# Eight stages without GpSimd's drain, one sort whose scatters are waited for once, and 57 of them in the gate instead of 60

## The chip, the cores and the metric

The kernel runs on one core of a Trainium2 chip. The metric is the device time of one execution in microseconds (us); lower is better. Five engines have programs of their own: PE (TensorE), DVE (VectorE), ACT (ScalarE), POOL (GpSimd) and SP (SyncE, which here only starts transfers).

## The reference, cut to what matters

The reference is a graph network of two layers over 3125 nodes of 256 features and 50,000 edges. Each layer adds to `x` a graph attention, a linear attention and an expert block:

```python
edge_index = jnp.stack([src, dst])
xn = _layernorm(x, axis=-1)
x = x + _L0_gnn_ref(xn, edge_index, edge_weight, ...) + _L0_mix_ref(xn[None], ...)[0]
x = x + _L0_ffn_ref(_layernorm(x, axis=-1)[None], ...)[0]      # 16 experts, 2 for each node
xn = _layernorm(x, axis=-1)
x = x + _L1_gnn_ref(xn, edge_index, ...) + _L1_mix_ref(xn[None], ...)[0]
x = x + _L1_ffn_ref(_layernorm(x, axis=-1)[None], ...)[0]      # 8 experts, 2 for all nodes
```

The graph attention of the first layer sums over the edges of a source node, that of the second over the edges of a destination node. So the edges are needed in two orders, and the kernel sorts them twice.

## The kernel before, in words

The kernel is eight stages, one after the other. Each stage is a function that opens one `nc.Block()`, in which every engine has a program, and closes it: `stage_project0` (p0), `stage_edges0` (e0), `stage_gate` (g), `stage_experts` (x), `stage_combine` (c), `stage_project1` (p1), `stage_edges1` (e1) and `stage_ffn1` (f). Nothing of a stage starts before all engines have ended the one before it. Names of tiles in the profile begin with the letter of the stage (`x_w` is `w` of `stage_experts`), and things that outlive a stage begin with `keep_` or `mid_`.

**What stands at a boundary.** In the compiled program the end of a block is this: PE, DVE, ACT and SP each drain (wait until their engine is idle) and report to a semaphore; GpSimd drains too, then waits for the four reports, and releases all. Then `Memory.release_semaphores` (L254 in the profile is its barrier) clears the semaphores of the stage, on GpSimd: a second drain, marked as a reset of this range of semaphores (`is_reset_sema`; the reset drain below), and the clear itself. A second barrier, of semaphores alone, follows. Then each engine branches to its program of the next stage.

**The two sorts.** An edge goes to its place by an indirect DMA of GpSimd: one DMA (a "scatter") takes one column `t` of the records, 128 edges, and writes each edge's record to the row of DRAM that `row` names. There are `EC` = 391 columns, so 391 scatters in a sort. `scatter_records` issues them in runs of `RUN` = 4 on two semaphores in turn; from the third run on a run waits until the last run on the same semaphore has landed, and at the end it waits until all have landed. The first sort (`sorted0`, records of four numbers) is wholly in p0, and e0 reads it. The second (`sorted1`, records of two) is read only by e1, and is cut in three: columns 0 to 59 (`SCATTERS_GATE` = 60) on GpSimd in g, where it has nothing else to do; columns 60 to 229 (`SCATTERS_EARLY` = 230) in x, behind the 50 scatters that send the rows of the nodes to their experts (L1321); columns 230 to 390 in p1. Each of the three calls has its own two semaphores, and ends with the wait for its own scatters.

**Orders within the stages.** In g, DVE works through normalising, the logits, the two best experts of each node and their places; its last instruction is L154, which writes `keep_expert_of`. In x, SP first loads the second weights (`x_w`, L215), then waits for the 50 scatters of GpSimd (`s_sent`), and only then loads the first tiles of rows (L1348). In e0 SP reads the sorted records first (L846); GpSimd's gathers (L863) need them. In e1 it is the same (L2097, L2120). GpSimd has no DMA in f.

Of the kernel before, what the change touches and what calls it, by code (L numbers as in the profile page):

```python
# [27 lines left out]
EC = -(-NE // P)  # L28
# [17 lines left out]
R1 = 4  # L46
assert R1 * TN >= G1_BINS
RUN = 4
SCATTERS_GATE = 60
SCATTERS_EARLY = 230  # L50
NOWHERE = 200.0

# [177 lines left out]
def scatter_records(pool, to, row, record, s_scat, begin, end):  # L230


    for n, t in enumerate(range(begin, end)):
        run = n // RUN
        if run >= 2 and n % RUN == 0:
            pool.wait_ge(s_scat[run % 2], 16 * RUN * (run // 2))
        pool.indirect_dma_start(  # L237
            out=to, out_offset=bass.IndirectOffsetOnAxis(ap=row[:, t:t + 1].bitcast(U32), axis=0),
            in_=record[:, t, :], in_offset=None).then_inc(s_scat[run % 2], 16)
    for half in range(2):  # L240
        pool.wait_ge(s_scat[half], 16 * sum(n // RUN % 2 == half for n in range(end - begin)))


class Memory:
# [32 lines left out]
def stage_project0(nc, a, k):  # L277
# [5 lines left out]
    with ExitStack() as ctx:  # L283
        m = Memory(nc, ctx, "p0")
# [86 lines left out]
        s_scat = [m.sem(f"scattered{i}") for i in range(2)]  # L371
# [28 lines left out]
        s_mixd = m.sem("mix_kept")  # L400
        s_v = m.sem("vector_steps")
        s_a = m.sem("scalar_steps")
        block = ctx.enter_context(nc.Block())

        @block.sync
        def _(sp):
# [31 lines left out]
        @block.gpsimd  # L438
        def _(pool):
            nc.gpsimd.iota(k["iota"][:], [[1, P]], base=0, channel_multiplier=0,  # L440
                           allow_small_or_imprecise_dtypes=True).then_inc(s_const, 1)
            nc.gpsimd.iota(iota_g[:], [[1, G1_N]], base=0, channel_multiplier=0,
                           allow_small_or_imprecise_dtypes=True).then_inc(s_const, 1)
            nc.gpsimd.iota(k["number"][:], [[0, 1]], base=0, channel_multiplier=1,
                           allow_small_or_imprecise_dtypes=True).then_inc(s_const, 1)
            nc.gpsimd.memset(k["ident"][:], 0.0).then_inc(s_const, 1)
            nc.gpsimd.memset(k["before"][:], 1.0).then_inc(s_const, 1)
            nc.gpsimd.memset(k["one"][:], 1.0).then_inc(s_const, 1)
            nc.gpsimd.iota(k["pairs"][:], [[1, TOPK * TN]], base=X_N * P - NP * TOPK * TN, channel_multiplier=TOPK * TN
                           ).then_inc(s_pad, 1)  # L450
            pool.wait_ge(s_const, 6)
            nc.gpsimd.affine_select(out=k["ident"][:], in_=k["ident"][:], compare_op=ALU.not_equal, fill=1.0, base=0,
                                    pattern=[[-1, P]], channel_multiplier=1).then_inc(s_const, 1)

            nc.gpsimd.affine_select(out=k["before"][:], in_=k["before"][:], compare_op=ALU.is_ge, fill=0.0, base=-1,
                                    pattern=[[1, P]], channel_multiplier=-1).then_inc(s_const, 1)
            nc.gpsimd.memset(zrow[:], 0.0).then_inc(s_pad, 1)

            pool.wait_ge(s_rows, 1)
            pool.wait_ge(s_fill, 64)  # L460
            scatter_records(pool, k["sorted0"], row0, record0, s_scat, 0, EC)

        @block.scalar
        def _(act):
# [317 lines left out]
def stage_edges0(nc, a, k):  # L782
# [7 lines left out]
    with ExitStack() as ctx:  # L790
        m = Memory(nc, ctx, "e0")
# [47 lines left out]
        s_agg = m.sem("added_up")  # L839
        s_acc = m.sem("accumulated")  # L840
        s_v = m.sem("vector_steps")
        block = ctx.enter_context(nc.Block())

        @block.sync
        def _(sp):
# [208 lines left out]
def stage_gate(nc, a, k):  # L1054


    with ExitStack() as ctx:
        m = Memory(nc, ctx, "g")
# [42 lines left out]
        s_base = m.sem("bases")  # L1101
        s_col = m.sem("bin_starts")
        s_row = m.sem("bin_starts_turned")
        s_scat = [m.sem(f"scattered{i}") for i in range(2)]
        s_v = m.sem("vector_steps")
        block = ctx.enter_context(nc.Block())

        @block.sync
        def _(sp):
# [3 lines left out]

        @block.gpsimd
        def _(pool):
            scatter_records(pool, k["sorted1"], k["row1"], k["record1"], s_scat, 0, SCATTERS_GATE)

        @block.scalar
        def _(act):
# [138 lines left out]
def stage_experts(nc, a, k):  # L1258
# [3 lines left out]
    with ExitStack() as ctx:  # L1262
        m = Memory(nc, ctx, "x")
# [27 lines left out]
        s_y = m.sem("y_made")  # L1291
        s_yk = m.sem("y_kept")
        s_out = [m.sem(f"tile_out{i}") for i in range(2)]
        s_scat = [m.sem(f"scattered{i}") for i in range(2)]
        block = ctx.enter_context(nc.Block())


        def turns(eng, step):
# [18 lines left out]
        @block.gpsimd  # L1317
        def _(pool):
            for r in range(TOPK):
                for t in range(TN):  # L1320
                    pool.indirect_dma_start(  # L1321
                        out=k["expert_in"], out_offset=bass.IndirectOffsetOnAxis(
                            ap=k["pairs"][:, r * TN + t:r * TN + t + 1].bitcast(U32), axis=0),
                        in_=k["all_rows"][:, t, :], in_offset=None).then_inc(s_sent, 16)


            scatter_records(pool, k["sorted1"], k["row1"], k["record1"], s_scat, SCATTERS_GATE, SCATTERS_EARLY)

        @block.sync
        def _(sp):  # L1330
# [119 lines left out]
def stage_combine(nc, a, k):  # L1450


    with ExitStack() as ctx:
        m = Memory(nc, ctx, "c")
# [13 lines left out]
        s_std = [m.sem(f"std{n}") for n in range(2)]  # L1468
        s_back = m.sem("scales_ready")
        s_v = m.sem("vector_steps")  # L1470
        block = ctx.enter_context(nc.Block())

        def columns(u):
            return range(u * TB, (u + 1) * TB)
# [124 lines left out]
def stage_project1(nc, a, k):  # L1599


    with ExitStack() as ctx:
        m = Memory(nc, ctx, "p1")
# [71 lines left out]
        s_num = m.sem("numerators")  # L1675
        s_att = m.sem("attention_rows")
        s_o = m.sem("outputs")
        s_scat = [m.sem(f"scattered{i}") for i in range(2)]
        s_v = m.sem("vector_steps")
        block = ctx.enter_context(nc.Block())  # L1680

        def row_of(t3, t):
            return t3[:, bass.ds(t, 1), :].rearrange("p a d -> p (a d)")
# [28 lines left out]
        @block.gpsimd  # L1712
        def _(pool):

            nc.gpsimd.memset(same[:], 1.0).then_inc(s_same, 1)
            view = same[:].rearrange("p (h d) -> p h d", h=HC)
            pool.wait_ge(s_same, 1)
            nc.gpsimd.affine_select(out=view, in_=view, compare_op=ALU.is_ge, fill=0.0, base=0,
                                    pattern=[[-MD, HC], [0, MD]], channel_multiplier=1).then_inc(s_same, 1)
            pool.wait_ge(s_same, 2)  # L1720
            nc.gpsimd.affine_select(out=view, in_=view, compare_op=ALU.is_ge, fill=0.0, base=MD - 1,
                                    pattern=[[MD, HC], [0, MD]], channel_multiplier=-1).then_inc(s_same, 1)

            scatter_records(pool, k["sorted1"], k["row1"], k["record1"], s_scat, SCATTERS_EARLY, EC)

        @block.scalar
        def _(act):
# [248 lines left out]
def stage_edges1(nc, a, k):  # L1976
# [7 lines left out]
    with ExitStack() as ctx:  # L1984
        m = Memory(nc, ctx, "e1")
# [78 lines left out]
        s_done = m.sem("averaged")  # L2064
        s_out = m.sem("written")
        s_v = m.sem("vector_steps")
        block = ctx.enter_context(nc.Block())

        def turns(eng, step, tail=(), enter=None, leave=None):

# [350 lines left out]
def stage_ffn1(nc, a, k, out):  # L2421


    with ExitStack() as ctx:
        m = Memory(nc, ctx, "f")
# [59 lines left out]
        s_res = m.sem("result_rows")  # L2485
        s_out = m.sem("written")
        s_v = m.sem("vector_steps")
        block = ctx.enter_context(nc.Block())

        def row_of(t3, t):  # L2490
            return t3[:, bass.ds(t, 1), :].rearrange("p a d -> p (a d)")
# [251 lines left out]
def build(nc, a, out):  # L2743

    with ExitStack() as ctx:
        def keep(name, shape, dt=F32):
            return ctx.enter_context(nc.sbuf_tensor(f"keep_{name}", shape, dt))

        def dram(name, shape):
            return nc.dram_tensor(f"mid_{name}", shape, F32, kind="Internal").ap()  # L2750

        k = {
            "x": keep("x", [NP, TN, D]),
            "iota": keep("iota", [P, P]),
            "number": keep("number", [P, 1]),
# [24 lines left out]
        with nc.sbuf_tensor("acc0", [P, TN, ROW], F32) as acc0:  # L2780
# [8 lines left out]
            with ExitStack() as layer:  # L2789
# [3 lines left out]
                stage_combine(nc, a, k)  # L2793
                stage_project1(nc, a, k)
        stage_edges1(nc, a, k)
        stage_ffn1(nc, a, k, out)

# [24 lines left out]
```

## Time and profile before

| | us |
|---|---|
| median of 3 runs | 3174.46 (3174.05 to 3175.06) |
| span of the profiled execution, first to last instruction | 3163.5 |
| median less span | 11.0 |
| stages (start of the first transfer of SP): e0, g, x, c, p1, e1, f | 638.93, 1246.13, 1343.95, 1720.44, 1824.03, 2137.26, 2867.91 |
| GpSimd busy | 1822.0 (58% of the span) |

The profile gives no time of the profiled execution beside its span; what lies around the span is taken as the 11.0 us between it and the median of the runs. Drains, barriers and waits are not counted as busy and have no rows of their own: they are seen as the distance from the last row of a stage to the first of the next. Times of rows are us from the start of the span.

### The profile page before, as it was taken

The numbers are of one execution on the slowest core, as the hardware profiler recorded it, in microseconds if no ns is written. First come the engines' busy times: TensorE is split into PE (matmuls) and PEld (weight loads), VectorE is DVE, ScalarE is ACT, GpSimd is POOL, SyncE is SP. The second block draws the span as 40 slices with busy tenths as digits, with TensorE's granted clock in tenths as the row PEclk, the third lists the DMA queues.
The fourth block names the chain that finished last, engine by engine and source line by source line (L and its number), as shares of the span: only waits on it lengthen the run. The fifth ranks groups of instructions, "written<-read, shape, count | busy, mean of one in ns | idle before, by whom it ended". The sixth has DMA issues, their size and how long they took to land. (4 is left out here: it accounts for less than half of the span.)

```text
span 3163.5 us, 53056 instructions
## 1 busy us (share of the span) xinstructions
PE 1683.1 (53%) x12473; PEld 1233.8 (39%) x12474; DVE 1885.3 (60%) x5563; ACT 816.7 (26%) x2575; POOL 1822.0 (58%) x1835
## 2 busy tenths in 40 slices
PE   0387544046666665409996078533444444321697
PEld 0154333035444443406664056422443334321465
DVE  6776799177777776402221922686777777665422
ACT  0144110024444442103332133001333333221232
POOL 0577777757777775677741477507777777710000
PEclk9998666568888875559998588765566656655899
DMA  3200000053333345053333200007444444842100
GB/s 111 97 22 18 2 1 2 2 194 106 106 103 106 106 102 54 1 204 82 86 85 104 60 18 17 11 0 139 105 104 106 105 105 104 86 40 81 30 16 24
DMA packets 169828, 225.16 MB, mean 71 GB/s; under 512 B 77729, under 2 KB 129096, under 8 KB 169639
## 3 DMA queue, kind: packets, MB, share of 16 engines
q0 software_dynamic: 74752, 140.02, 20.3%
q1 hardware_dynamic: 95012, 84.45, 9.2%
q8 instruction: 20, 0.33, 0.0%
q14 instruction: 44, 0.36, 0.0%
HBM read 185.16 MB, written 39.18 MB: 71 GB/s over the span
## 5 line engine op out<-in xcount | busy, mean ns | idle before, releaser
L2120 POOL DMA_INDIRECT e_rows<-mid_table,e_rec x488 | 487.8, 1000 | 258.1 <-issue 137.4
L237 POOL DMA_INDIRECT mid_sorted<-p_record,p_row x391 | 404.2, 1034 | 224.8 <-issue 122.4
L863 POOL DMA_INDIRECT e_rows<-mid_table,e_rec x448 | 433.9, 969 | 157.8 <-issue 99.0
L237 POOL DMA_INDIRECT mid_sorted<-keep_record,keep_row x391 | 396.6, 1014 | 145.9 <-issue 122.8
L1023 PE MATMUL e_ps_A<-e_rows,e_hot 128*125 128x260 f32 x896 | 329.8, 503 | 0.0
L2376 PE MATMUL e_ps_mT<-keep_ident,e_marked 128*128 128x128 f32 x488 | 118.3, 424 | 198.9 <-DVE e_marked L2144 198.9
L1023 PEld LDWEIGHTS e_ps_A<-e_rows,e_hot 128*125 128x125 f32 x896 | 202.2, 250 | 28.1
L2338 ACT ACTIVATE e_acc<-e_state 128x66 f32 x488 | 126.1, 258 | 259.3 <-ACT e_acc L2338 217.0
L1008 PE MATMUL e_ps_T<-e_identb,e_hot 128*125 128x128 bf16 x454 | 89.5, 289 | 191.4 <-DVE e_hot L884 190.2
L1384 DVE COPY x_hidden<-x_ps_h 128x512 f32<-128x512 f32 x64 | 44.2, 691 | 230.3 <-PE x_ps_h L1413 230.3
L2376 PEld LDWEIGHTS e_ps_mT<-keep_ident,e_marked 128*128 128x128 f32 x488 | 95.7, 223 | 203.4 <-issue 203.4
L2144 DVE TENSOR_TENSOR e_marked<-e_hot,e_rows 128x1024 f32<-128x1024 bf16 x61 | 74.8, 1225 | 156.9 <-DMA e_rows<-mid_table,e_rec 156.7
L904 DVE TENSOR_TENSOR e_rows<-e_rows 128x512 f32<-128x512 f32 x224 | 153.1, 684 | 1.7 <-ACT e_rows L988 1.4
L1413 PE MATMUL x_ps_h<-w,x_xT 128*128 x256 | 129.7, 630 | 14.7 <-ACT x_xT L1362 14.5
L1008 PEld LDWEIGHTS e_ps_T<-e_identb,e_hot 128*125 128x125 bf16 x454 | 53.5, 166 | 211.6 <-DVE e_hot L884 210.3
L2171 DVE SCALAR_TENSOR_TENSOR e_state<-e_state,e_scale,e_ps_A 128x65 f32<-128x65 f32 x488 | 134.9, 277 | 0.7 <-issue 0.2
L1429 PE MATMUL x_ps_y<-x_w,x_hT 128*128 x512 | 122.3, 382 | 1.7 <-ACT x_hT L1369 1.7
L137 DVE TENSOR_TENSOR_SCAN p_running<-p_ones,p_first,p_mask 128x391 f32<-128x391 f32 x125 | 118.8, 1012 | 5.3 <-DVE p_mask L134 5.3
L980 ACT ACTIVATE acc<-e_state 125x260 f32 x224 | 94.0, 420 | 101.6 <-DVE e_state L912 100.7
L884 DVE TENSOR_SCALAR e_hot<-keep_iota,e_rec 128x125 f32<-128x125 f32 x454 | 116.1, 353 | 1.1
L1429 PEld LDWEIGHTS x_ps_y<-x_w,x_hT 128*128 128x128 f32 x512 | 95.9, 190 | 45.0 <-issue 31.3
L777 PE MATMUL p_ps_mix<-p_kw,p_qvT 128*125 128x256 f32 x100 | 51.0, 664 | 115.7 <-DVE keep_x L689 114.7
(520 smaller groups left out, 4078.6 us busy)
## 6 DMA issues: line engine op xcount, KB each, us to landing
e_rows<-mid_table,e_rec POOLq DMA_INDIRECT x936
mid_expert_in<-p_zrow SPq DMA_DIRECT2D x1, 8192.0 KB
w<-in_L_ffn_w SPq DMA_DIRECT2D x16, 512.0 KB
x_w<-in_L_ffn_w SPq DMA_DIRECT2D x16, 512.0 KB
x_xs<-mid_expert_in SPq DMA_DIRECT2D x64, 128.0 KB
x_b<-in_L_ffn_b SPq DMA_DIRECT2D x64, 128.0 KB
mid_expert_out<-x_y SPq DMA_DIRECT2D x64, 128.0 KB
mid_sorted<-p_record,p_row POOLq DMA_INDIRECT x391
```

The costliest lines, as they stand in the source:

```text
L137: o.done(o.eng.tensor_tensor_scan(runnings[:, j], one, masks[:, j], first[:, bass.ds(b + j, 1)], ALU.mult, ALU.add))
L237: pool.indirect_dma_start(out=to, out_offset=bass.IndirectOffsetOnAxis(ap=row[:, t:t + 1].bitcast(U32), axis=0), in_=record[:, t, :], in_o ...
L863: pool.indirect_dma_start(out=rows[:, s % RING * 2 + j, :], out_offset=None, in_=k["table"], in_offset=bass.IndirectOffsetOnAxis(ap=rec[:, ...
L904: nc.vector.tensor_tensor(r, r, spread(w, P, 2, H, HD), ALU.mult).then_inc(s_wm, 1)
L1008: last = nc.tensor.transpose(ps_T[q % 2][0:NP, j, 0:P], halves[:, :, 1], identb[:])
L1023: last = nc.tensor.matmul(ps_A[0:NP, q % 4, 0:ROW], hot[:, q * 2 + j, :], rows[:, q * 2 + j, :], start=j == 0, stop=j == 1)
L1413: last = nc.tensor.matmul(ps_h[q % 2][:], xT[:, q % 2, c, :], k["w1"][:, bass.ds(e, 1), c, :].rearrange("p a f -> p (a f)"), start=c == 0, ...
L1429: last = nc.tensor.matmul(ps_y[q % 2][:], hT[:, c, :], w2[:, bass.ds(e, 1), c, :].rearrange("p a d -> p (a d)"), start=c == 0, stop=c == F ...
L2120: pool.indirect_dma_start(out=rows[:, j, q, :], out_offset=None, in_=k["table1"], in_offset=bass.IndirectOffsetOnAxis(ap=rec[:, i * TG + q ...
L2171: v.scalar_tensor_tensor(state[:, j, q, 0:W1], before, scale[:, j, q:q + 1], sums_of(j)[:, q // HALF, q % HALF * W1:(q % HALF + 1) * W1], ...
L2338: nc.scalar.activation(acc[:, bass.ds(block_of, 1), :].rearrange("p a w -> p (a w)"), state[:, j, q, :], ACT.Copy).then_inc(s_keep, 1)
L2376: last = nc.tensor.transpose(ps_mT[:, q // HALF, q % HALF * P:(q % HALF + 1) * P], marked[:, q, :], k["ident"][:])
```

## The change

Three things are done. All eight blocks are opened with `no_gpsimd_drain=True`: the other engines drain as before, GpSimd does not, and the barrier is the one of semaphores alone. The two semaphores of the second sort are allocated once for the whole kernel (`k["s_scat1"]`) and cleared at its very end, with one more barrier; a run is counted by the column, `t // RUN`, so that the counts go on from stage to stage, and the wait for all scatters (`scatters_landed`) stands only behind the last part, in p1. The first sort keeps its wait in p0. And the gate gets 57 scatters, so the experts' stage gets 173 where it had 170.

```diff
-SCATTERS_GATE = 60
+SCATTERS_GATE = 57
...
 def scatter_records(pool, to, row, record, s_scat, begin, end):
-    for n, t in enumerate(range(begin, end)):
-        run = n // RUN
-        if run >= 2 and n % RUN == 0:
+    for t in range(begin, end):
+        run = t // RUN
+        if run >= 2 and t % RUN == 0:
             pool.wait_ge(s_scat[run % 2], 16 * RUN * (run // 2))
         pool.indirect_dma_start(
...
+def scatters_landed(pool, s_scat):
     for half in range(2):
-        pool.wait_ge(s_scat[half], 16 * sum(n // RUN % 2 == half for n in range(end - begin)))
+        pool.wait_ge(s_scat[half], 16 * sum(t // RUN % 2 == half for t in range(EC)))
...
# in each of the eight stages:
-        block = ctx.enter_context(nc.Block())
+        block = ctx.enter_context(nc.Block(no_gpsimd_drain=True))
...
# stage_project0
             scatter_records(pool, k["sorted0"], row0, record0, s_scat, 0, EC)
+            scatters_landed(pool, s_scat)
...
# stage_gate
-            scatter_records(pool, k["sorted1"], k["row1"], k["record1"], s_scat, 0, SCATTERS_GATE)
+            scatter_records(pool, k["sorted1"], k["row1"], k["record1"], k["s_scat1"], 0, SCATTERS_GATE)
...
# stage_experts
-            scatter_records(pool, k["sorted1"], k["row1"], k["record1"], s_scat, SCATTERS_GATE, SCATTERS_EARLY)
+            scatter_records(pool, k["sorted1"], k["row1"], k["record1"], k["s_scat1"], SCATTERS_GATE, SCATTERS_EARLY)
...
# stage_project1
-            scatter_records(pool, k["sorted1"], k["row1"], k["record1"], s_scat, SCATTERS_EARLY, EC)
+            scatter_records(pool, k["sorted1"], k["row1"], k["record1"], k["s_scat1"], SCATTERS_EARLY, EC)
+            scatters_landed(pool, k["s_scat1"])
...
# build
+        s_scat1 = [nc.alloc_semaphore(f"keep_scattered{i}") for i in range(2)]
...
         stage_ffn1(nc, a, k, out)
+        nc.clear_and_free_semaphores(s_scat1)
+        nc.all_engine_barrier(sem_only=True)
```

## Rows read from the trace of the kernel before

**Rows 1.** The page's first line.
```profile
span 3163.5 us, 53056 instructions
```

**Rows 2.** The chain that ended last, its first piece: start, us, what.
```profile
2867.91 0.27 SPq L2498
```

**Rows 3.** Timeline, p0 to e0: start, us, engine, line, what, idle before.
```profile
562.62 0.36 DVE L694 CAST keep_row<-p_running 128x391 int32<-128x391 f32 x1
...
631.11 0.96 POOL L237 DMA_INDIRECT mid_sorted<-p_record,p_row  x1 [0.30 <-issue]
638.93 0.37 SPq L846 DMA_DIRECT2D e_rec<-mid_sorted  x1
...
646.41 0.99 POOL L863 DMA_INDIRECT e_rows<-mid_table,e_rec  x1 [14.34 <-DVE e_rec L917]
```

**Rows 4.** Timeline, g to x.
```profile
1332.24 0.95 POOL L237 DMA_INDIRECT mid_sorted<-keep_record,keep_row  x1 [0.30 <-issue]
...
1333.99 0.21 DVE L154 TENSOR_SCALAR keep_expert_of<-g_ps_T 1x66 int32<-1x66 f32 x1 [0.47 <-PE g_ps_T L163]
...
1336.03 0.96 POOL L237 DMA_INDIRECT mid_sorted<-keep_record,keep_row  x1 [0.30 <-issue]
1343.95 0.29 SPq L1331 DMA_DIRECT2D x_beta<-in_L_ffn_beta  x1
...
1344.63 0.96 POOL L1321 DMA_INDIRECT mid_expert_in<-acc,keep_pairs  x1 [7.65 <-POOLq L254]
```

**Rows 5.** Timeline, e0 to g.
```profile
1244.59 0.42 ACT L980 ACTIVATE acc<-e_state 125x260 f32 x1 [1.23 <-DVE e_state L912]
1246.13 0.37 SPq L215 DMA_DIRECT2D g_gw<-in_L_ffn_gate_w  x1
...
1246.80 1.00 POOL L237 DMA_INDIRECT mid_sorted<-keep_record,keep_row  x1 [23.04 <-POOLq L254]
```

**Rows 6.** Timeline, the four later boundaries.
```profile
1721.15 0.97 POOL L1498 DMA_INDIRECT c_yk<-mid_expert_out,keep_pairs  x1 [94.66 <-PEq L1453]
...
1820.32 2.56 ACT L1514 ACTIVATE acc<-keep_x,c_back,c_rstd 125x256 f32<-125x256 f32 x5 [0.46 <-DVE c_back L1576]
...
1823.55 0.20 POOL L1715 MEMSET p_same<- 128x128 f32 x1 [39.14 <-POOLq L254]
...
2129.62 6.82 DVE L1877 TENSOR_TENSOR keep_x<-keep_x,acc 125x6400 f32<-125x6400 f32 x1
2137.26 0.37 SPq L2097 DMA_DIRECT2D e_rec<-mid_sorted  x1
...
2142.88 7.70 POOL L2120 DMA_INDIRECT e_rows<-mid_table,e_rec  x1 [108.05 <-DVE e_rec L2227]
...
2779.69 1.02 POOL L2120 DMA_INDIRECT e_rows<-mid_table,e_rec  x1 [0.30 <-issue]
```

**Rows 7.** DMA traffic, 630 to 638 us, in 40 slices of 0.2 us.
```profile
GB/s 7 4 0 0 0 0 3 7 0 0 0 0 0 11 0 0 0 0 0 0 0 0 0 0 0 0 0 0 0 0 0 0 0 0 0 0 0 0 0 0
```

**Rows 8.** The same, 1334 to 1342 us.
```profile
GB/s 0 0 0 0 0 5 0 0 0 0 0 4 1 0 0 0 0 2 3 0 0 0 0 0 0 0 0 0 0 0 0 0 0 0 0 0 0 0 0 0
```

**Rows 9.** Timeline, the end of the sends in x and what waits for them.
```profile
1406.61 0.96 POOL L1321 DMA_INDIRECT mid_expert_in<-acc,keep_pairs  x1 [0.30 <-issue]
...
1409.84 0.35 SPq L1348 DMA_DIRECT2D x_xs<-mid_expert_in  x1
...
1413.61 0.66 PE L1406 MATMUL x_ps_x<-keep_ident,x_xs 128*128 128x128 f32 x2 [79.66 <-DMA x_b<-in_L_ffn_b]
```

**Rows 10.** DMA traffic there, 1404 to 1411 us, in 40 slices of 0.175 us.
```profile
GB/s 0 23 374 328 24 0 0 0 0 351 351 47 0 0 0 0 304 304 141 0 0 0 0 187 351 211 0 0 0 0 1 5 0 0 0 0 0 0 6 194
```

**Rows 11.** What is known of the scatters' landing (view of the tile `mid_sorted`).
```profile
DMA to landing us min/median/max: 2.1/2.1/5.6
```

**Rows 12.** Timeline of g: two of the scatters that took longer.
```profile
1248.10 7.33 POOL L237 DMA_INDIRECT mid_sorted<-keep_record,keep_row  x1 [0.30 <-issue]
...
1324.14 2.38 POOL L237 DMA_INDIRECT mid_sorted<-keep_record,keep_row  x1 [0.30 <-issue]
```

More of the change, by code:

```diff
@@ L841, in stage_edges0 @@
         s_v = m.sem("vector_steps")
-        block = ctx.enter_context(nc.Block())
+        block = ctx.enter_context(nc.Block(no_gpsimd_drain=True))
         @block.sync
@@ L1103, in stage_gate @@
         s_row = m.sem("bin_starts_turned")
-        s_scat = [m.sem(f"scattered{i}") for i in range(2)]
         s_v = m.sem("vector_steps")
-        block = ctx.enter_context(nc.Block())
+        block = ctx.enter_context(nc.Block(no_gpsimd_drain=True))
         @block.sync
@@ L1293, in stage_experts @@
         s_out = [m.sem(f"tile_out{i}") for i in range(2)]
-        s_scat = [m.sem(f"scattered{i}") for i in range(2)]
-        block = ctx.enter_context(nc.Block())
+        block = ctx.enter_context(nc.Block(no_gpsimd_drain=True))
         def turns(eng, step):
@@ L1470, in stage_combine @@
         s_v = m.sem("vector_steps")
-        block = ctx.enter_context(nc.Block())
+        block = ctx.enter_context(nc.Block(no_gpsimd_drain=True))
         def columns(u):
@@ L1677, in stage_project1 @@
         s_o = m.sem("outputs")
-        s_scat = [m.sem(f"scattered{i}") for i in range(2)]
         s_v = m.sem("vector_steps")
-        block = ctx.enter_context(nc.Block())
+        block = ctx.enter_context(nc.Block(no_gpsimd_drain=True))
         def row_of(t3, t):
@@ L2066, in stage_edges1 @@
         s_v = m.sem("vector_steps")
-        block = ctx.enter_context(nc.Block())
+        block = ctx.enter_context(nc.Block(no_gpsimd_drain=True))
         def turns(eng, step, tail=(), enter=None, leave=None):
@@ L2487, in stage_ffn1 @@
         s_v = m.sem("vector_steps")
-        block = ctx.enter_context(nc.Block())
+        block = ctx.enter_context(nc.Block(no_gpsimd_drain=True))
         def row_of(t3, t):
@@ L2750, in dram @@
             return nc.dram_tensor(f"mid_{name}", shape, F32, kind="Internal").ap()
+        s_scat1 = [nc.alloc_semaphore(f"keep_scattered{i}") for i in range(2)]
         k = {
+            "s_scat1": s_scat1,
             "x": keep("x", [NP, TN, D]),
```

## The prediction

> **What bounds the kernel now.** The span is 3163.5 us [rows 1]. The chain of waits begins only at 2867.91 [rows 2]: it doesn't reach back over the last boundary, so it tells nothing of this change. I read the boundaries in the timeline instead, for at each the whole chip stands still. The question at each is which engine came last, and how long after it the next stage began.
>
> At five of the seven boundaries GpSimd had long been done. From e0 to g ACT ends last, at 1244.59 + 0.42 = 1245.01, and SP starts at 1246.13, 1.12 us later; GpSimd, which idled 23.04 us, starts at 1246.80 [rows 5]. From c to p1 ACT ends at 1822.88 and GpSimd starts at 1823.55, 0.67 us later, after 39.14 us idle. From p1 to e1 DVE ends at 2136.44 and SP starts 0.82 us later. At the start of c GpSimd had idled 94.66 us; its last gather of e1 ends at 2780.71, 87 us before f [rows 2, 6]. So a boundary in which GpSimd came early costs 0.7 to 1.1 us, with both barriers, the reset drain and the clear in it.
>
> At two boundaries GpSimd comes last. In p0 DVE is done at 562.98, GpSimd's last scatter ends at 631.11 + 0.96 = 632.07, and SP starts at 638.93: 6.86 us of nothing [rows 3]. In g DVE is done at 1333.99 + 0.21 = 1334.20, the last scatter ends at 1336.99, and SP starts at 1343.95, 6.96 us after it and 9.75 after DVE [rows 4]. The two distances are the same, though 391 scatters stand behind the one and 60 behind the other. Each is three things: the last scatter lands, GpSimd drains, the barriers pass.
>
> **How much of the 6.86 is the drain.** The barriers are 1.12 [rows 5]. Landing: the last traffic of p0 lies in the fourteenth slice, 632.6 to 632.8, then nothing moves [rows 7]; in g the last lies at 1337.4 to 1337.8 and then nothing [rows 8]. So the data is down 0.7 us after GpSimd's row ends. The semaphore comes later. A neighbour says how much: the last send ends on GpSimd at 1407.57 [rows 9], its data moves until about 1408.55 [rows 10], and SP, which waits for it, loads at 1409.84, after reading the tile's expert [rows 9]. That is 1.3 us from data to the load, of which I estimate 0.4 for SP's reading: 0.9. By this the scatter has landed 0.7 + 0.9 = 1.6 us after its row, and the drain is 6.86 - 1.6 - 1.12 = 4.1 us. Bounds: data alone, 0.7, gives 5.0; the median landing of 2.1 [rows 11], counted from the row's end, gives 3.6.
>
> Here the trace goes against a rule. No byte moves from 632.8 to 638.93, and yet the chip stands [rows 7]. The Trainium skill (PSUM — Partial Sum Buffer, "Engine vs sequencer instructions") says that a drain waits for the engine to go fully idle. By that alone a drain behind a wait for everything that GpSimd issued would be free, and the first boundary would gain nothing; its time is worked out below from rows, as the first rival.
>
> **The change, part by part.**
> *The drain goes at p0 to e0.* The wait for the landing stays, so only the drain's 4.1 us go (3.6 to 5.0). Everything of e0 hangs on the barrier: SP's load of the records, then GpSimd's first gather at 646.41 [rows 3]. All of it moves up.
>
> *At g to x drain and wait go, and three scatters.* The 57th scatter starts at 1332.24 and ends at 1333.19 [rows 4], 1.0 us before DVE. Without landing and drain GpSimd is at the barrier first, and DVE sets the end: 1334.20 + 0.82 (DVE last, as at p1 to e1 [rows 6]) = 1335.0 in place of 1343.95. That is 8.9 us; by the 1.12 of rows 5 it is 8.6. I take 8.8. What could spoil it is the pace of the scatters. Two of g's long ones are 7.33 and 2.38 us [rows 12], where DVE was at work; if GpSimd fell 2.1 us further behind (two such short stalls), it would end at 1335.3 and the gain would be 7.5. So 7.5 to 9.1.
> The 8.8 carries on. In x GpSimd's 50 sends start 0.68 us after SP [rows 4], SP loads rows only when they have landed, and PE waits 79.66 us for that [rows 9]; weights and sends all hang on the barrier and move together.
>
> *Three more scatters in x* are 3 x 1.26 us (1332.24 to 1336.03 for three [rows 4]) = 3.8 us on GpSimd, queued behind the sends. They are covered by the 94.66 us that GpSimd idles at the end of x [rows 6]; without this cover they would cost their 3.8. The waits inside the runs now count by column: column 60, the fourth of x, waits for runs that were issued before 50 sends. Cost nothing. The same holds in p1, where GpSimd idles some 100 us at the end [rows 6].
>
> *The drain goes at the other six block ends.* It ran while GpSimd idled 23 us or more [rows 5, 6], and in f GpSimd has no DMA. Nothing, within 0.1 us each.
>
> *The last clear and barrier* are new, behind the last block: something like half a boundary. A whole one is 0.67 to 1.12 [rows 5, 6]; I take 0.5 us, with 0 and 1.1 as bounds.
>
> Sum: -4.1 - 8.8 + 0.5 = -12.4 us. The profiled execution would go from 3163.5 to 3150.6 in span, with the last clear outside it. Its own time is the span plus the 11.0 around it, 3174.5, the median; so 3174.5 - 12.4 = **3162.1 us**. Bounds: -(3.6 + 7.5) + 1.1 = -10.0, and -(5.0 + 9.1) = -14.1, so 3160.4 to 3164.5.
>
> **The rivals.**
> *1. The drain is cheap, the landing long.* This is the rule above as a mechanism. The longest known landing is 5.6 us [rows 11]; behind the last scatter it would reach 637.67, and 1.12 for the barriers gives 638.79, almost SP's start. Then the first boundary gains 0.1 us. The second still gains 8.8, since its wait for landing goes too. Total -0.1 - 8.8 + 0.5 = -8.4: 3166.1 us. Against it: twice the same distance, where landing is 2.1 in the median.
>
> *2. The reset drain takes over, at every boundary (slower).* The reset drain comes behind the first barrier, where nothing covers it. Before, it always found GpSimd's DMAs retired by a plain drain. If the price of the plain drain is this retiring, the reset drain now pays it in all seven stages with DMAs of GpSimd: 7 x 4.1 = 28.7 against the 12.4 gained, +16.3: 3190.8 us. It decides from 12.4 / 7 = 1.8 us a boundary; from 0.86 (7 x 0.86 = 6.0) the gain is under 0.2%. For it: the reset drain's cost without a plain drain in front is seen nowhere. Against: the distance doesn't grow from 60 to 391 scatters [rows 3, 4], so it isn't a retiring one by one; and a reset need not wait.
>
> *3. The reset drain takes over only behind fresh DMAs.* Where GpSimd has just issued, at p0 to e0 and g to x, the price stays: nothing is gained at the first, and at the second 4.1 comes back behind the barrier, 8.8 - 4.1. Total -4.7 + 0.5 = -4.2: 3170.3 us, within the noise bound. For it: the price was seen at just these two. It is the form in which the change does not do what it says.
>
> **How the numbers follow.** Of the sum as worked out 0.64; rival 1 0.12; rival 2 0.12; rival 3 0.10; 0.02 for something unlisted and faster. About 0.2% of 3174.46, 6.35 us, is what a measurement of this kernel can tell from no change. Under 3168.1 lie the sum, rival 1 and the rest: faster 0.78; same 0.10; slower 0.12. The likeliest alone is 3160.4 to 3164.5. The range takes in rivals 1 and 3 and leaves out rival 2: 3160 to 3171.
>
> **What the profile after would show.** SP's L846 4.1 us earlier against the last scatter: some 2.7 us behind its end in place of 6.86. SP's first load of x 0.8 to 1.1 us behind DVE's L154, and 57 scatters ending before it. The other five distances unchanged at 0.7 to 1.1 us: were they 2 us or more longer, rival 2 holds. If only the first distance is unchanged, rival 1; if x starts 5 us behind DVE, rival 3. The prediction would also be wrong if g's scatters ran at another pace and ended behind DVE, or if a stage stretched by what its start gained.

## The result and the profile after

The changed kernel takes 3158.06 us (median of 4 runs, 3157.63 to 3159.42), the kernel before in the same comparison 3174.76 (3174.05 to 3177.52). The ratio is 0.9946, 95% interval 0.9932 to 0.9960: 17.1 us less, with 12.7 to 21.6 in the interval. The interval leaves no change out: it is faster, as forecast, but below the range of 3160 to 3171.

The page's first line, and p0 to e0 in the timeline of the changed kernel (start, us, engine, line, what, idle before):

```profile
span 3155.9 us, 53088 instructions
```

```profile
560.02 0.36 DVE L699 CAST keep_row<-p_running 128x391 int32<-128x391 f32 x1
...
639.56 0.96 POOL L237 DMA_INDIRECT mid_sorted<-p_record,p_row  x1 [0.30 <-issue]
642.77 0.37 SPq L851 DMA_DIRECT2D e_rec<-mid_sorted  x1
...
650.20 1.00 POOL L868 DMA_INDIRECT e_rows<-mid_table,e_rec  x1 [9.68 <-DVE e_rec L922]
```

From the last scatter's end, 640.52, to SP's load it is 2.25 us where it was 6.86 [rows 3]: 4.61 less. But the last scatter itself ends 8.4 us later than it did, with DVE 2.6 us earlier, although nothing in p0 changed ahead of it. e0 begins 3.8 us later than before. More on this below.

The 6.86 us can also be read directly. I had written that drains have no rows; the timeline leaves them out, but the view of a line (`--source`, durations in ns: shortest/median/longest) has them. Of the kernel before, the drain at the end of p0 and of g, and the eight reset drains; then the eight reset drains of the changed kernel:

```profile
L283 POOLq DRAIN  x1: 4559/4559/4559, 633.5 to 633.5; - x1
L1057 POOLq DRAIN  x1: 4945/4945/4945, 1338.3 to 1338.3; - x1
L253 POOLq DRAIN  x8: 81/93/129, 638.2 to 3162.8; - x8
```

```profile
L257 POOLq DRAIN  x8: 67/90/130, 642.1 to 3155.1; - x8
```

The plain drain of p0 starts 1.41 us behind the last scatter's end, when the wait for the landing is over, and takes 4.56; SP's load comes 0.89 us behind it. In g it takes 4.95. The reset drain takes some 0.1 us in all eight blocks, before the change and after it.

The same for e0 to g, and for g to x:

```profile
1247.52 0.42 ACT L985 ACTIVATE acc<-e_state 125x260 f32 x1 [1.31 <-DVE e_state L917]
1248.78 0.37 SPq L215 DMA_DIRECT2D g_gw<-in_L_ffn_gate_w  x1
...
1249.78 1.00 POOL L237 DMA_INDIRECT mid_sorted<-keep_record,keep_row  x1 [24.55 <-issue]
```

```profile
1334.91 0.96 POOL L237 DMA_INDIRECT mid_sorted<-keep_record,keep_row  x1 [0.30 <-issue]
...
1336.67 0.21 DVE L154 TENSOR_SCALAR keep_expert_of<-g_ps_T 1x66 int32<-1x66 f32 x1 [0.47 <-PE g_ps_T L163]
1337.68 0.28 SPq L1334 DMA_DIRECT2D x_beta<-in_L_ffn_beta  x1
...
1338.34 0.96 POOL L1324 DMA_INDIRECT mid_expert_in<-acc,keep_pairs  x1 [2.46 <-POOLq L258]
```

GpSimd's 57th scatter ends at 1335.87, DVE at 1336.88, and SP starts 0.80 us later, where it was 9.75 after DVE [rows 4]. g, from SP's first load to SP's first load of x, lasts 88.90 us in place of 97.82: 8.92 less. From e0 to g, where GpSimd was early, it is 0.84 us in place of 1.12 [rows 5]; from c to p1 0.71 in place of 0.67, and from p1 to e1 0.89 in place of 0.82 [rows 6].

Stage by stage (start to start, by SP's first transfer; f to the end of the span):

| stage | before | after | difference |
|---|---|---|---|
| p0 | 638.93 | 642.77 | +3.84 (scatters +8.45, drain -4.61) |
| e0 | 607.20 | 606.01 | -1.19 |
| g | 97.82 | 88.90 | -8.92 |
| x | 376.49 | 376.90 | +0.41 |
| c, p1 | 103.59, 313.23 | 103.70, 313.39 | +0.11, +0.16 |
| e1 | 730.65 | 729.46 | -1.19 |
| f | 295.6 | 294.8 | -0.8 |
| span | 3163.5 | 3155.9 | -7.6 |

The spans differ by only 7.6 us, the medians by 16.7. That was the first thing to clear up: the changed kernel's profiled execution took 3157.66 us, 1.8 more than its span, where I had put 11.0 us around the span of before.

### The profile page after: what moved, and what is told of

Read it like the earlier page. It is cut to its first block and busy times, and to the rows that moved or that the text cites. A ratio compares the mean times of both kernels' runs of the same rounds, so it can differ in the third digit from the quotient of the medians.

```text
span 3155.9 us, 53088 instructions
## 1 busy us (share of the span) xinstructions
PE 1678.4 (53%) x12473; PEld 1230.1 (39%) x12474; DVE 1890.9 (60%) x5563; ACT 817.2 (26%) x2575; POOL 1829.8 (58%) x1835
## 5 line engine op out<-in xcount | busy, mean ns | idle before, releaser
L237 POOL DMA_INDIRECT mid_sorted<-p_record,p_row x391 | 412.0, 1054 | 225.4 <-issue 123.0
```

Of the source, the lines that this page charges most:

```text
L237: pool.indirect_dma_start(out=to, out_offset=bass.IndirectOffsetOnAxis(ap=row[:, t:t + 1].bitcast(U32), axis=0), in_=record[:, t, :], in_o ...
```

## The experiments

**1. What lies around the span, and does f's drain pay it?** Three variants and the kernel before itself, on one chip. `f_only` sets the option on the last block alone:

```diff
 # stage_ffn1 of the kernel before
-        block = ctx.enter_context(nc.Block())
+        block = ctx.enter_context(nc.Block(no_gpsimd_drain=True))
```

`after_f_drained` is the changed kernel with this edit turned round; `p0_only` is the kernel before with the edit in `stage_project0` alone.

> The kernel before, once more, for the span and the time of the same executions. Theory A (what lies around the span, 11.0 us before and 1.8 us after the change, is set by the program): time less span is 11.0 +- 0.3 in every run. Theory B (it was an accident of the one comparison, a span from one execution and a time from others): it varies by several us. For p0's scatters: if their pace is an accident of an execution, the last one ends anywhere between 632 and 641 us; if it is set by the program, within 1 us of 632.07, and the spans of all runs agree with 3163.5 within 1.5.

> The kernel before, with the option on the last block (f) alone. Theory F (the 9.2 us around the span are the drain of GpSimd in f, where GpSimd has no DMA and no work; it is paid behind the last row): the span stays 3163.5 +- 1.5 and the time falls by 9 us to 3165.5. Theory L (they are the last clear and barrier that the change adds, which f_only has not): nothing moves, 3174.5. Theory S (the end pays something for every block that drained GpSimd, once): f_only gets a seventh or an eighth of it, 1.2 us, 3173.3.

> The changed kernel, with the plain drain put back in the last block alone. Theory F: 9.2 us come back, outside the span: 3158.1 + 9.2 = 3167.3, span 3155.9 +- 1.5. Theory L: nothing comes back, 3158.1. Theory S: 1.2 us, 3159.3.

> The kernel before, with the option on the first block (p0) alone; the wait for the landing of the scatters stays in it. The distance from the last scatter's end to SP's first load of e0 was 6.86 before and 2.25 after the change. Theory D (the drain is 4.6 us): the distance is 2.25. Rival: the distance shrank since the scatters of p0 ended later against DVE, not by the drain: it stays 6.9. For the pace: if the option slows p0's own scatters (their last ended 8.4 us later after the change), the last ends at about 640 and the time is 3174.5 - 4.6 + 8.4 = 3178.3; if the slower pace has another cause, the last ends at 632 and the time is 3169.9.

Measured, against 27 runs of the kernel before (median 3171.55, 3165.58 to 3177.72):

| kernel | median us (runs) | ratio | 95% interval | time less span, each run |
|---|---|---|---|---|
| before_again | 3170.50 (10) | 0.9998 | 0.9988 to 1.0009 | 1.7 |
| f_only | 3173.52 (11) | 0.9998 | 0.9989 to 1.0008 | 1.7 to 1.8 |
| after_f_drained | 3157.16 (5) | 0.9947 | 0.9934 to 0.9961 | 1.7 to 1.8 |
| p0_only | 3168.19 (11) | 0.9990 | 0.9981 to 0.9999 | 1.7 to 1.8 |

Theory A falls: around the span there are 1.7 to 1.8 us, in every run of every kernel. Theory B had the right reason, a span of one execution set against a time of others, but what it expected of time less span, several us of variation, isn't so. The drain in f (theories F and S) is worth nothing, and so are the last clear and barrier of theory L to within the noise. The profile of before was of one execution, and its span of 3163.5 makes that one of some 3165.2 us, at the very low end of what this kernel does.

One reason for the spread stands in p0 (last scatter, SP's first load of e0), in before_again and p0_only:

```profile
635.81 0.96 POOL L237 DMA_INDIRECT mid_sorted<-p_record,p_row  x1 [0.31 <-issue]
643.63 0.37 SPq L846 DMA_DIRECT2D e_rec<-mid_sorted  x1
```

```profile
637.82 0.95 POOL L237 DMA_INDIRECT mid_sorted<-p_record,p_row  x1 [0.31 <-issue]
641.04 0.37 SPq L846 DMA_DIRECT2D e_rec<-mid_sorted  x1
```

In the same kernel the last scatter now ends at 636.77 in place of 632.07. Over twelve profiles of all kernels that leave p0's scatters alone it ends anywhere from 632.07 to 642.94, with and without the change. So the pace, which I had offered as either an accident or set by the program, differs from execution to execution of one program. The distance behind it does not: it is 6.86 again in before_again, 2.27 in p0_only. The drain's 4.6 us stand; the time of p0_only, 3.4 us less with 0.3 to 6.0 in its interval, holds them but is too coarse to show them.

**2. Do the two places add up, and is that all?** `after_again`, `after_third` and `after_fourth` are the changed kernel; `g_only` and `g_only_b` have the plain drain back in all blocks but g, `two_places` in all but p0 and g (the edit of part 1, turned round).

> The changed kernel, once more. The distances at the boundaries gave 4.61 us at p0 to e0 and 8.92 in g, 13.5 together; the medians of the first comparison differ by 16.7 and the 95% interval of their ratio reaches from 12.7 to 21.6 us. Theory C (13.5 is all, the rest is chance: the last scatter of p0 ended anywhere from 632.1 to 642.9 in six profiled executions, of kernels whose p0 has the same instructions up to the drain): the ratio over more runs is 0.9957 (13.5 us), and the two distances are 2.25 and 0.8 again. Rival (the change gives 3 us more somewhere): 0.9947 with an interval that leaves 0.9957 out.

> The changed kernel with the plain drain back in seven blocks; only g ends without it, and the shared semaphores and the 57 scatters stay. If the two places add up, this keeps the 8.9 us of g and loses the 4.6 of p0: SP's first load of x 0.8 us behind DVE's L154, SP's first load of e0 6.86 us behind the last scatter, time 3171.5 - 8.9 = 3162.6. Rival (what the drain does is carried from stage to stage, so that one plain drain later or earlier changes g's end): g's length is not 88.9 us.

> The changed kernel, a third time, since the chip of the second time was another case (there p0 ended with SP, 390 us behind GpSimd). On a chip where the kernel before takes some 3170 us, theory C (4.61 us at p0 to e0 and 8.92 in g are all) expects a ratio of 0.9957 with an interval that holds it; the rival (3 us more somewhere) 0.9947 with an interval that leaves 0.9957 out. The two distances: 2.25 and 0.8 us.

> The changed kernel with the plain drain back in seven blocks; only g ends without it. If the two places add up, g lasts 88.9 us as in the changed kernel, SP's first load of e0 is 6.86 us behind the last scatter, and the ratio is 1 - 8.9 / 3173 = 0.9972. Rival: g's length is not 88.9, or the ratio's interval leaves 0.9972 out.

> The changed kernel beside g_only_b on the same chip. Theory C (the boundaries are all): ratio 0.9957, and g_only_b lies 4.6 us above it. Rival (some 3 us more, in f or elsewhere): ratio 0.9947 or lower. In f the four profiles of the changed kernel gave 294.8 to 296.0 us from its first load to the span's end, those of the kernel before and its variants 295.6 to 298.1; theory C says that this is chance.

> The changed kernel with the plain drain back in the six blocks other than p0 and g. Theory C (p0's and g's ends are all that the change gives by itself): p0 to e0 2.25 us, g 88.9 us, ratio 0.9957. On the clock in f: in f's loop the five profiles of the changed kernel and its variants without drains show the granted clock at 1.00 throughout, the eight others one or two falls to 0.50 of some 3.4 us. If the drains of the other stages are behind that, two_places shows such falls; if it goes by what p0 and g end like, none; if by chance, either.

| kernel | median us | before, same chip | ratio | 95% interval | p0 to e0 | g |
|---|---|---|---|---|---|---|
| after_third | 3164.48 | 3176.51 | 0.9958 | 0.9944 to 0.9973 | 2.25 | 88.90 |
| after_fourth | 3160.67 | 3177.34 | 0.9944 | 0.9929 to 0.9958 | 2.25 | 88.91 |
| g_only_b | 3168.13 | 3177.34 | 0.9970 | 0.9956 to 0.9984 | 6.84 | 88.88 |
| after_again | 4312.34 | 4316.25 | 0.9993 | 0.9984 to 1.0002 | (see below) | 142.7 |
| g_only | 4319.56 | 4316.25 | 1.0008 | 0.9999 to 1.0017 | (see below) | 142.7 |
| two_places | 4311.84 | 4308.66 | 1.0003 | 0.9994 to 1.0012 | (see below) | 142.6 |

g_only_b gives g's part by itself: 0.9970, which is 9.5 us, against 8.9 expected. Beside after_fourth it lies 7.5 us higher, where 4.6 were expected. The distances agree to 0.02 us in every profile. 13.5 us (0.9957) lies in the interval of each of the three comparisons of the changed kernel, and so does 0.9947; their mean is 0.9949, 16 us, and after_f_drained has 0.9947 too. If the four comparisons are taken as independent, the interval of their mean is some +-0.0007 (my estimate, half of that of each), with 13.5 us at its edge. No single time settles it; the profiles of f, below, say more.

Seven runs (these three, and after_60, two_drains, counts_a and counts_b below) fell where the kernel before takes 4309 to 4316 us, in loops where PE waits up to 43 us for nothing that the profile shows. I call this the odd chip, but what makes it so isn't known: four of the seven bear the number 14, and the other three the number 5, which the runs of part 1 bear as well, where the kernel before took 3171.55. They are no measure of the 13.5, but they teach one thing. In after_again DVE ends p0 at 1020.1, 391 us behind GpSimd's last scatter, and in g DVE comes last too, so both drains are covered there. The gain at a boundary belongs to the places where GpSimd comes last, not to the drain. The ratios of the changed kernel there, 0.9993 and 0.9992 (after_60, 0.9983 to 1.0001), leave some 3 us that no boundary explains, with no change just inside their intervals. On the odd chip the three scatters are not free either: with 57 in g, g lasts 142.6 to 142.7 us and x 589.5 to 590.5 (three profiles), with 60 in g it is 146.7 to 146.9 and 586.0 to 586.7 (four).

**3. What are g's 8.9 us made of?** `after_60` (on the odd chip) and `after_60_b` are the changed kernel with `SCATTERS_GATE = 60`. `waits_dropped` has plain drains and 60 scatters, but the shared semaphores, so g doesn't wait for its scatters:

```diff
 # the changed kernel
-SCATTERS_GATE = 57
+SCATTERS_GATE = 60
 # waits_dropped also, in all eight blocks:
-        block = ctx.enter_context(nc.Block(no_gpsimd_drain=True))
+        block = ctx.enter_context(nc.Block())
```

> The changed kernel with 60 scatters in the gate. Theory G (whoever comes last sets g's end): GpSimd ends three scatters of 1.26 us later, 2.8 us behind DVE, and g lasts 88.9 + 2.8 = 91.7 us. Rival (GpSimd as the last one costs more than DVE as the last one, since the reset drain then stands right behind fresh DMAs): 91.7 and something, 96 if it is the whole 4.6. The whole is too small for the time to tell; g's length is what counts.

> The changed kernel with 60 scatters in the gate. Theory G (whoever comes last sets g's end): GpSimd ends 2.8 us behind DVE, g lasts 91.7 us. Rival (GpSimd as the last costs more, its reset drain standing right behind fresh DMAs): up to 96.

> The kernel before (60 scatters, plain drains in all blocks) with the shared semaphores, so that g no longer waits for its scatters to land; only the drain stands between the last scatter and the barrier. Theory D (the drain's price of 4.6 starts when it is reached, and runs beside the landing): the distance from the last scatter to SP's first load of x falls from 6.96 by the landing, some 1.4, to 5.6. Rival W (the drain waits for the landing and then takes its 4.6): the distance stays 6.9 us and the wait in the code was worth nothing while the drain stood.

The timelines of g's end, after_60_b and then waits_dropped:

```profile
1336.32 0.95 POOL L237 DMA_INDIRECT mid_sorted<-keep_record,keep_row  x1 [0.31 <-issue]
...
1337.77 0.28 SPq L1334 DMA_DIRECT2D x_beta<-in_L_ffn_beta  x1
...
1338.42 0.96 POOL L1324 DMA_INDIRECT mid_expert_in<-acc,keep_pairs  x1 [1.15 <-POOLq L258]
```

```profile
1337.71 0.96 POOL L237 DMA_INDIRECT mid_sorted<-keep_record,keep_row  x1 [0.30 <-issue]
1344.31 0.29 SPq L1334 DMA_DIRECT2D x_beta<-in_L_ffn_beta  x1
```

Without drain and wait SP starts 0.50 us behind GpSimd's last scatter; with the drain alone 5.64 (expected 5.6); with drain and wait 6.96 [rows 4]. So in g the drain is 5.14 us, the wait for the landing 1.32. g lasts 91.39 us in after_60_b (91.7 expected), 96.52 in waits_dropped and 97.85 in the drained g of two_drains_b on the same chip, and 88.90 with 57 scatters: drain 5.1, landing 1.3, three scatters 2.5. after_60 gave g 146.9 on its chip, where DVE came last (1885.9, SP 1886.8), and says nothing of this.

The 0.50 us also settle the rivals with the reset drain. It stands right behind fresh scatters, and behind 899 DMAs that no plain drain ever followed, and costs nothing that can be seen; in the changed kernel its eight rows are 0.07 to 0.13 us long, and in g of after_60_b its row ends 0.08 us behind the last scatter's.

**4. What does the drain's price go by?** `two_drains` and `two_drains_b` put one more `nc.gpsimd.drain()` behind p0's wait; the other three put drains between the scatters of the first sort, in the kernel before:

```diff
         if run >= 2 and n % RUN == 0:
             pool.wait_ge(s_scat[run % 2], 16 * RUN * (run // 2))
+        if end - begin == EC and n in (10, 40, 90, 160, 250, 370):     # counts_a
+            pool.drain()
```

> The kernel before with one more plain drain on GpSimd in p0, behind the wait for the scatters and ahead of the block's own. Theory P (a plain drain of GpSimd has a fixed price, whatever is outstanding): the distance from the last scatter to SP's first load of e0 goes from 6.86 to 6.86 + 4.6 = 11.5 us. Rival R (the price is that of retiring what is outstanding, and the second finds nothing): 6.86 to 7.2 us.

> One more plain drain on GpSimd in p0 of the kernel before, behind the wait. Theory P (fixed price): the distance from the last scatter to SP's first load of e0 is 11.5 us in place of 6.86. Rival R (retiring what is outstanding): 6.86 to 7.2 us.

> The kernel before, with plain drains of GpSimd put between scatters of the first sort, where their price stands in the idle time ahead of the next scatter's row (0.30 us without one): one drain ahead of scatter 100, one ahead of 104, two ahead of 120; a wait for all landed and one drain ahead of 140; the wait alone ahead of 160. Theory Q (the first drain behind a DMA costs 4.6 to 5.1 us, whatever has landed and however many DMAs there were; one behind another is free): idle 5.4 at 100, 104 and 120, 6.3 at 140, 1.7 at 160. Rival N (it goes by the number of DMAs since the last drain): much at 100, little at 104. Rival E (the price is of a block's end, not of the drain): 0.3 to 1.5 everywhere.

> The kernel before, with one plain drain of GpSimd ahead of scatters 10, 40, 90, 160, 250 and 370 of the first sort, so 10, 30, 50, 70, 90 and 120 scatters after the last one, and 21 ahead of the block's own. mid_drains gave idle times of 2.08, 2.66 and 8.95 us after 4, 16 and 100 scatters. Theory N (a drain goes through what was issued since the last one, some 0.07 us each on top of 1.5): idle 2.4, 3.8, 5.2, 6.6, 8.0 us, and 10 after 120, unless it starts anew somewhere past 100: the block ends, with 251 scatters behind mid_drains' last drain and 391 before, cost only 2.3 and 4.6. Theory Q (fixed): all the same. The block's own, after 21 with the landing waited for: 6.86 - 4.6 + 2 = 4.5 us from the last scatter to SP's load.

> The same with one drain after 110 scatters and one after 140 more; 141 ahead of the block's own. Theory N without a limit: idle 9.5 and 11.6 us, and 12 us from the last scatter to SP's load. Theory N with a restart past some 100: one or both of the later ones fall to 2 to 5 us.

two_drains_b, p0 to e0: 6.76 us from 637.83, so the second drain is free. (The rows were 4.56 us for the first and 0.03 for the second.)

```profile
636.87 0.96 POOL L237 DMA_INDIRECT mid_sorted<-p_record,p_row  x1 [0.31 <-issue]
644.59 0.37 SPq L847 DMA_DIRECT2D e_rec<-mid_sorted  x1
```

two_drains fell on the odd chip, where p0 doesn't end with GpSimd, but its two drains have rows too:

```profile
L462 POOLq DRAIN  x1: 9882/9882/9882, 631.4 to 631.4; - x1
L283 POOLq DRAIN  x1: 41/41/41, 641.3 to 641.3; - x1
```

Here the first one took 9.88 us, behind the same 391 landed scatters that cost 4.56 elsewhere. The second is free again. The rows of the scatters right behind a drain, in mid_drains, with the idle time in brackets that was 0.30 without one: ahead of scatter 100, 104, 120 (two drains) and 140 (landing waited for as well):

```profile
241.68 0.96 POOL L243 DMA_INDIRECT mid_sorted<-p_record,p_row  x1 [8.95 <-issue]
248.51 0.96 POOL L243 DMA_INDIRECT mid_sorted<-p_record,p_row  x1 [2.08 <-issue]
271.19 0.95 POOL L243 DMA_INDIRECT mid_sorted<-p_record,p_row  x1 [2.66 <-issue]
299.98 0.96 POOL L243 DMA_INDIRECT mid_sorted<-p_record,p_row  x1 [3.76 <-issue]
```

In counts_a, behind 10, 30, 50, 70, 90 and 120 scatters:

```profile
120.22 0.96 POOL L239 DMA_INDIRECT mid_sorted<-p_record,p_row  x1 [2.29 <-issue]
161.02 0.96 POOL L239 DMA_INDIRECT mid_sorted<-p_record,p_row  x1 [3.22 <-issue]
228.67 0.96 POOL L239 DMA_INDIRECT mid_sorted<-p_record,p_row  x1 [4.85 <-issue]
323.22 0.95 POOL L239 DMA_INDIRECT mid_sorted<-p_record,p_row  x1 [6.48 <-issue]
448.09 0.96 POOL L239 DMA_INDIRECT mid_sorted<-p_record,p_row  x1 [11.54 <-issue]
609.04 0.96 POOL L239 DMA_INDIRECT mid_sorted<-p_record,p_row  x1 [8.56 <-issue]
```

In counts_b, behind 110 and 140:

```profile
254.90 0.96 POOL L239 DMA_INDIRECT mid_sorted<-p_record,p_row  x1 [9.77 <-issue]
442.28 0.96 POOL L239 DMA_INDIRECT mid_sorted<-p_record,p_row  x1 [10.93 <-issue]
```

Less the 0.30, the price is 1.8 us after 4 scatters, 2.0 after 10, 2.4 after 16, 2.9 after 30, 4.6 after 50, 6.2 after 70, 8.7 after 100, 9.5 after 110 and 10.6 after 140. From 30 to 110 these lie within 0.02 us of 0.45 us and 0.082 for each scatter since the last drain. (counts_a and counts_b fell on the odd chip; the 100 are of mid_drains, which did not.) The fixed price that I held in mid_drains falls. Two points lie off, 11.2 after 90 and 8.3 after 120, and so does 140, where the line has 11.9. The first points hold a landing as well: the wait for it alone, ahead of scatter 160 of mid_drains, took 1.64 us.

Drains behind a wait, with everything landed, can be read from their own rows (`--source` of the block's line), on the odd chip too:

| DMAs since the last drain | in | drain, us | drain on the odd chip, us |
|---|---|---|---|
| 20 | mid_drains, ahead of scatter 140 | 1.67 | |
| 21 | counts_a, end of p0 | | 1.76 |
| 60 | end of g | 4.94 to 4.95 | 4.94 to 4.95 |
| 141 | counts_b, end of p0 | | 7.17 |
| 161 | end of p1 | 4.04 to 4.21 | 4.05 to 6.21 |
| 220 (50 of them sends) | end of x | 4.78 to 4.79 | 11.86 to 11.92 |
| 251 | mid_drains, end of p0 | 2.25 | |
| 391 | end of p0 | 4.56 | 9.68 to 9.88 |

20, 21 and 60 are 0.083 us each. From 141 on the number of DMAs doesn't set the price: the same 220 cost 4.8 us or 11.9. What does was not tried. So landing adds to a short drain, but the greater part of the price stands with all landed.

**The rest of the gain: TensorE's clock in f.** The loop of f is matmuls with four long pauses, in each of which PE waits for ACT's `f_hT`. The stretches behind such a pause, by windows (length, busy time of PE, PEld, DVE, ACT and POOL, granted clock, DMA, GB/s), in before and in before_again, and the loop of the changed kernel from 2955 on (its first 4 us or so are at 0.50 in every profile):

```profile
3086.00:3090.00 4.00, 4.00 (x10) 2.70 (x10) 0.29 (x1) 1.10 (x3) 0.00 (x0) 0.60 0.22 76
3090.00:3150.00 60.00, 55.35 (x232) 42.47 (x230) 13.58 (x38) 12.14 (x21) 0.00 (x0) 1.00 0.04 16
```

```profile
3012.00:3018.00 6.00, 5.04 (x12) 3.40 (x13) 1.41 (x4) 2.21 (x5) 0.00 (x0) 0.72 0.21 70
...
3091.00:3096.00 5.00, 4.41 (x10) 2.96 (x11) 1.05 (x3) 1.70 (x4) 0.00 (x0) 0.66 0.19 68
```

```profile
2955.00:3140.00 185.00, 173.57 (x700) 128.26 (x699) 47.58 (x121) 50.86 (x89) 0.00 (x0) 1.00 0.04 14
```

Right behind a pause the granted clock falls to its lower level (0.50, 1.2 GHz) for some 3.4 us, once in before, twice in before_again, never in after. Sixteen matmuls there take 6.14 us, the same sixteen 4.67 at 1.00 (2.4 GHz). PE's timeline, before and then after, with the pause in brackets:

```profile
3085.84 6.14 PE L2718 MATMUL f_ps_h<-f_xT,f_w 128*128 x16 [1.89 <-ACT f_hT L2545]
```

```profile
3079.49 4.67 PE L2721 MATMUL f_ps_h<-f_xT,f_w 128*128 x16 [1.81 <-ACT f_hT L2548]
```

All twenty profiles, those of the odd chip too, divide into the same two groups:

| | profiles | falls of the clock | pauses, us | first matmul of `f_ps_h` to last of `f_ps_y` |
|---|---|---|---|---|
| no plain drain in e0, x, c, p1, e1: after, after_f_drained, after_third, after_fourth, after_60_b, after_60, after_again | 7 | none | 1.60, then 1.80 to 1.81 | 193.3 to 193.9 |
| with it: before and all others, two_places and g_only among them | 13 | one to three | 1.89 to 1.90 | 194.8 to 197.9 |

Off the odd chip the means are 193.6 and 195.8 us, so f is 2.2 us shorter. two_places was to tell whether the drains of the other blocks are behind it. It shows a fall, and pauses of 1.89 to 1.90 us, and after_again and after_60 on the odd chip show neither. With twenty profiles on one side or the other, chance is no longer a good account. f_only and after_f_drained say that f's own drain is not, p0_only and g_only that those of p0 and g are not.

The pause is shorter before the clock has fallen anywhere, since PE comes to it later. In the changed kernel PE waits for ACT just ahead of the first long pause:

```profile
2998.37 2.35 PE L2721 MATMUL f_ps_h<-f_xT,f_w 128*128 x8 [0.26 <-ACT f_hT L2548]
3002.32 2.87 PE L2721 MATMUL f_ps_h<-f_xT,f_w 128*128 x9 [1.60 <-ACT f_hT L2548]
```

In before PE doesn't wait there, and this pause is longer by about what the wait took (the later ones by 0.1 us):

```profile
3008.68 1.50 PE L2718 MATMUL f_ps_h<-f_xT,f_w 128*128 x4 [1.90 <-ACT f_hT L2545]
```

ACT starts the instruction in question 50.32 us behind f's first matmul in after and 50.02 in before, with the matmuls up to there at the same times. Why a drain of GpSimd stages earlier moves it by 0.3 us isn't shown, nor that the longer pause is what lets the clock fall. Another edit that moves ACT's program without touching a drain was not tried.

## Why the prediction was wrong, step by step

- *What bounds the boundaries, and who comes last*: right. GpSimd was last at two of seven, and only these two moved.
- *The drain at p0 to e0, 4.1 us (3.6 to 5.0)*: 4.61, in its bounds. By the rows of before the three parts of the 6.86 are 1.41 for the landing, where I had 1.6, 4.56 for the drain, and 0.89 for the barriers, where I took 1.12 from a boundary that ends with ACT.
- *g to x, 8.8 us (7.5 to 9.1)*: 8.92, in its bounds. DVE sets the end at 0.80 us, and the scatters kept their pace. (Two stalls like the 2.38 us of rows 12 would be 2.8 us and not 2.1; none came.)
- *Three more scatters in x at nothing*: x lasts 376.9 us, inside the 374.6 to 377.1 of the other profiles. Right here, though not on the odd chip.
- *The drain at the other six block ends: "Nothing, within 0.1 us each"*: this is the step that failed. It is right at the boundaries: e0 to g went from 1.12 to 0.84. But I looked for a price only where the drain stands. The seven profiles without the drains of e0, x, c, p1 and e1 have no fall of the clock in f, the thirteen with them have one to three, and f's loop is 2.2 us shorter in the mean (0.9 to 3.7 by single profiles off the odd chip). With this term at nothing the measured sizes of the others give 3174.5 - 4.6 - 8.9 + 0.2 = 3161.2, inside the range; with it 3159.0, below. What links those drains to f stays open.
- *The last clear and barrier, 0.5*: from SP's last transfer to the span's end 8.03 in place of 7.83: 0.2 us.
- *The base and the range*: "Its own time is the span plus the 11.0 around it" is false. It is the span plus 1.7, and the profiled execution was one of some 3165.2 us, 9 below the median. This didn't move the forecast, for the base was the median all the same, and that held: 3174.76 in the comparison. But the median came of three runs that agreed within 1.0 us, and I took that for this kernel's spread; 27 more runs reach over 12 us. A range built from the bounds of the terms alone, 3160 at its low end, had no room for it.
- *What is left*: the measured time of 3158.06 is 4.1 below the forecast. 0.9 are the sizes of the terms (4.6 for 4.1, 8.9 for 8.8, 0.2 for 0.5), 2.2 are f by the mean of its profiles, and 1.0 is within what chance does between four runs and three.
- *Rival 1 (cheap drain, long landing)*: dead; the landing is 1.3 to 1.4 us. p0_only, which takes only the drain away, shows it at 4.6 us with everything landed. The Trainium skill (PSUM — Partial Sum Buffer, "Engine vs sequencer instructions") has a drain wait for the engine to go fully idle. I had read that as free once all is landed, and the measurement decides against this reading; whether GpSimd is idle by the page's meaning in those 4.6 us no row shows.
- *Rivals 2 and 3 (the reset drain takes over)*: dead by the 0.50 us of after_60_b. But my argument against rival 2 was bad. "The distance doesn't grow from 60 to 391 scatters, so it isn't a retiring one by one": it does grow with each scatter, by 0.082 us from 30 to 110, and stops doing so past that. 60 and 391 happened to cost alike and hid it. The work is not passed on to the reset drain all the same.

## What to carry to other kernels

At a boundary between stages ask who comes last; a drain, a wait or a transfer costs only there. On GpSimd a plain drain behind 20 to 391 indirect DMAs took 1.7 to 11.9 us here even when all had landed, so where a semaphore already proves the landing, or nothing reads the data yet, it can go; and work that fills a gap is to be cut so that it ends just ahead of the engine that sets the stage's end. Before a forecast is set against a median, look at how far whole executions differ: one span is one draw. And an edit that can't cost anything where it stands can still move a later stage: compare every stage over several profiles, not only the ones that were touched.

## What the runs showed that I had not expected

- A plain drain of GpSimd costs 0.082 us for each scatter since the last one, from 30 to 110 scatters, and less than that line at 251 (2.3) and 391 (4.6, or 9.7 to 9.9 on the odd chip). A second drain behind it is free (0.03 to 0.05 us).
- With GpSimd last, both barriers, the reset drain and the clear take 0.50 us; with DVE last 0.80.
- 391 scatters, the same program, take 527 to 537 us from the first one's start at 105.5 to the last one's end (mean of a scatter 1034 ns in before, 1044 in before_again, 1054 in after). Why is not shown.
- Behind four pauses of 1.89 to 1.90 us TensorE's granted clock fell to 0.50 in some turns of the loop and not in others (22 of 52 in thirteen profiles), behind those of 1.60 to 1.81 us in none of 28. Which it is goes by whether five earlier blocks end with GpSimd's drain.
- The kernel before took 4309 to 4316 us beside seven of the runs, in place of 3171 to 3177, and the change was worth 0.07% there.
